# Macaron block: VectorE's routing passes spread over more units, low parts of two groups of units on other engines, three weight pieces ahead

## What is computed

```python
x = x + 0.5 * ffn(layernorm(x))      # x: 2048 tokens x 128
x = x + attention(layernorm(x))
x = x + 0.5 * ffn(layernorm(x))

def ffn(x):                           # 64 experts, D = 128, F = 64
    shared = silu(x @ Ws_up) @ Ws_down
    aff = x @ centroids.T
    _, idx = top_k(aff + expert_biases, 8)
    w = sigmoid(take(aff, idx)); w = w / (sum(w) + 1e-8)
    cw = zeros(T, 64) with w at idx
    h = silu(einsum('td,edf->etf', x, W_up))
    y = einsum('etf,efd->etd', h, W_down)
    return shared + einsum('etd,te->td', y, cw)

def attention(x):                     # one head of 128, 2048 x 2048 logits
    q, k, v = x @ Wq, x @ Wk, x @ Wv
    return (softmax(q @ k.T) / sqrt(128)) @ v
```

## Time and profile before

| what | us |
|---|---|
| median of 3 runs | 564.39 (564.20 to 564.67) |
| the profiled execution, its own time | 564.02 |
| its span, first to last instruction | 562.2 |
| PE busy | 536.9 (95%) |
| VectorE busy | 409.1 (73%) |
| ScalarE busy | 411.1 (73%) |
| GpSimd busy | 274.5 (49%) |
| granted TensorE clock, mean | 0.993 |

### The profile page before, as it was taken

How to read it: one execution, slowest core, us unless ns; L and a number is a source line. 1 busy time by engine, 2 the same in 40 slices (tenths; PEclk the granted TensorE clock), 3 DMA queues, 4 the chain that set the end, 5 groups by cost and what they waited for, 6 DMA issues and landing times.

```text
span 562.2 us, 8626 instructions
## 1 busy us (share of the span) xinstructions
PE 536.9 (95%) x2683; PEld 436.3 (78%) x2683; DVE 409.1 (73%) x920; ACT 411.1 (73%) x814; POOL 274.5 (49%) x242
## 2 busy tenths in 40 slices
PE   7699999899989999999999999899999999999997
PEld 5476887688778887679999999777787788778885
DVE  5478678867876775676778979687777967875664
ACT  7688877777787786666666656677877787787774
POOL 3897675676676675100000000064775666567563
PEclk9799999999999999999999999999999999999999
DMA  8544664455446562000000000054565466466652
GB/s 267 178 152 149 196 206 154 149 181 169 147 149 196 183 192 60 0 1 2 1 2 0 2 1 1 2 158 151 178 198 178 150 193 189 145 183 196 196 189 97
DMA packets 44270, 72.25 MB, mean 129 GB/s; under 512 B 8864, under 2 KB 9632, under 8 KB 44224
## 3 DMA queue, kind: packets, MB, share of 16 engines
q1 hardware_dynamic: 43568, 71.17, 39.7%
q10 hardware_dynamic: 592, 0.39, 0.2%
q0 software_dynamic: 64, 0.13, 0.1%
HBM read 69.57 MB, written 2.10 MB: 127 GB/s over the span
## 4 chain that ended last, share of the span: by engine, by line
PE 76%; DVE 9%; ACT 6%; issue 4%; POOL 3%; DMA 1%; POOLq 0%; SPq 0%; DVEq 0%; ACTq 0%
PE lrow L1044 11%; PE lrow L1045 11%; PE lrow L1046 11%; PE bank L1082 9%; PE bank L1084 8%; PE bank L1083 8%; PE bank L1116 6%; PE bank L1316 3%; PE bank L1318 3%; PE bank L1317 3%; ACT gpart_hi L437 2%; DVE rec L754 2%; ACT lrow L426 1%; POOL gpart_lo L273 1%; DVE gpart_lo L273 1%
## 5 line engine op out<-in xcount | busy, mean ns | idle before, releaser
L273 POOL TENSOR_TENSOR gpart_lo<-gated,gpart_hi 128x512 fp32r<-128x512 f32 x174 | 224.9, 1295 | 183.3 <-ACT gpart_hi L437 179.3
L426 ACT ACTIVATE lrow<-lrow 128x512 f32<-128x512 f32 (+1 forms) x246 | 143.6, 584 | 60.3 <-PE lrow L1046 60.1
L670 DVE TENSOR_TENSOR gated<-lrow,wide 128x512 f32<-128x512 f32 x166 | 114.2, 688 | 47.9 <-ACT lrow L426 44.8
L437 ACT CAST gpart_hi<-gated 128x512 fp32r<-128x512 f32 x174 | 106.7, 614 | 13.1 <-DVE gated L670 12.6
L1082 PE MATMUL bank<-gpart_lo,wdn_hi 128*128 128x512 f32 x256 | 102.3, 399 | 5.7 <-POOL gpart_lo L273 5.7
L1084 PE MATMUL bank<-gpart_hi,wdn_hi 128*128 128x512 f32 x256 | 101.8, 398 | 0.0
L1083 PE MATMUL bank<-gpart_hi,wdn_lo 128*128 128x512 f32 x256 | 101.3, 396 | 0.0
L670 DVE TENSOR_TENSOR lrow<-lrow,wide 128x512 f32<-128x512 f32 x78 | 54.3, 696 | 41.6 <-ACT lrow L426 41.3
L1082 PEld LDWEIGHTS bank<-gpart_lo,wdn_hi 128*128 128x128 f32 x256 | 48.3, 189 | 19.4 <-issue 5.6
L979 DVE TENSOR_TENSOR pT_lo<-bank,pT_hi 128x512 fp32r<-128x512 f32 x64 | 43.7, 684 | 25.7 <-ACT pT_hi L614 25.7
L273 DVE TENSOR_TENSOR gpart_lo<-lrow,gpart_hi 128x512 fp32r<-128x512 f32 (+1 forms) x84 | 57.4, 683 | 2.5 <-ACT gpart_hi L437 1.8
(11 more groups left out here) (239 smaller groups left out, 943.6 us busy)
## 6 DMA issues: line engine op xcount, KB each, us to landing
wide<-gates_dram SPq DMA_DIRECT2D x488, 128.0 KB, 3.0
raw<-in_w_up SPq DMA_DIRECT2D x8, 256.0 KB, 5.5
raw<-in_w_down SPq DMA_DIRECT2D x8, 256.0 KB, 5.7
gates_dram<-gates SPq DMA_DIRECT2D x8, 128.0 KB, 2.3
x<-in_x SPq DMA_DIRECT2D x3, 256.0 KB, 3.6
out_dram<-x SPq DMA_DIRECT2D x3, 256.0 KB, 2.9
x<-in_x SPq DMA_DIRECT2D x1, 128.0 KB, 2.7
x<-in_x ACTq DMA_DIRECT2D x1, 128.0 KB, 2.9
```

The source lines that it names most:

```text
L273: return eng.tensor_tensor(gpart[1][0:m, U % NGP, :], gated_at(U)[0:m, :], gpart[0][0:m, U % NGP, :].bitcast(F32), ALU.subtract)
L426: nc.scalar.activation(dst[0:m, :], hid[U % NH][0:m, :], ACT.Silu).then_inc(s_silu, 1)
L437: nc.scalar.copy(gpart[0][0:m, U % NGP, :], gated_at(U)[0:m, :]).then_inc(s_ghi, 1)
L670: nc.vector.tensor_tensor(gated_at(U), a, b, ALU.mult).then_inc(s_gated, 1)
```

## The change

- **First chunk.** `PRE` is 3, so three weight pieces are made ahead and the others at units 0, 2, ... 24. ScalarE makes a unit's conversion before the piece in the same step, and piece 2 before the gates' copy. In chunk 0 up to unit 24, `on_pool` gives GpSimd only units 7, 9, ... 23; VectorE makes the low parts of units 0 to 6 and of the even ones. The small products for attention's weights come three units later.
- **Routing passes.** The reciprocal is two halves of two token tiles each, behind `pro_aff` at unit 14 and behind unit 15's gate; GpSimd's `weights` waits for both through a new semaphore. `joint_lo` moves from unit 15 to 24. Attention's normalisation moves from units 17 and 18 to 20 and 21, with its scratch in the free down bank. kT's steps move from 22 and 23 to 26 and 27, qT's from 26 and 27 to 30, 31 and 32, the values from 24 to 27, and attention's `rstd` on GpSimd from 14 to 12.
- **Unit 15** of every chunk has its low part on GpSimd.

```diff
-PRE = 6
+PRE = 3
@@ on_pool
-            return u % 3 != 0 and (u < UNITS - 1 or n % NCH < NCH - 1)
+            if n == 0 and u < 25:
+                return u > EARLY and u % 2 == 1
+            return u == 15 or u % 3 != 0 and (u < UNITS - 1 or n % NCH < NCH - 1)
@@ GpSimd
+                pool.wait_ge(p_rec, 2 * joint(n))
                 pool.wait_ge(p_top, n + 1)
...
-                        if f == 0 and c and u == 14:
+                        if f == 0 and c and u == 12:
                             rstd(1, c - 1, e_st, e_rs)
-                        if f == 0 and c and u == 24:
+                        if f == 0 and c and u == 27:
                             value_parts(c - 1)
@@ ScalarE
+                            piece_hi(2)
                             pro_cwT(n)
-                            piece_hi(2)
                             silu_unit(3, n)
-                            for k in range(3, PRE):
-                                piece_hi(k)
...
+                        if c or u > 1 - f:
+                            hi_unit(*before(u, n))
                         if n == 0 and u % 2 == 0 and PRE + u // 2 < 2 * WP:
                             piece_hi(PRE + u // 2)
-                        if c or u > 1 - f:
-                            hi_unit(*before(u, n))
@@ VectorE
+                free = yacc[n % 2] if k else mp
+                ve, t, r = (free[:, TPC * E + i * TPC:TPC * E + (i + 1) * TPC] for i in range(3))
...
+            def reciprocal(n, half):
+
+                dve.wait_ge(p_affs, n)
+                some = slice(half * GT, (half + 1) * GT)
+                nc.vector.reciprocal(rec[:, some, :], aff[n // NCH][:, some, :]).then_inc(p_rec, 1)
...
                                 pro_aff(n + 1, 1)
+                                reciprocal(n + 1, 0)
                             if u == 15:
-                                pro_top(n + 1, 0)
+                                reciprocal(n + 1, 1)
+                            if u == 24:
                                 joint_lo(n + 1)
...
-                                if u == 17:
+                                if u == 20:
...
-                                if u == 18:
+                                if u == 21:
                                     normed(1, c - 1, c - 1, xn2, e_rs, e_xn, (2, 3))
-                                if u == 23:
+                                if u == 27:
                                     epi_lo(c - 1)
-                                if u == 27:
+                                if u == 32:
                                     epi_proj_lo(c - 1)
@@ TensorE
-                                if u == 22:
+                                if u == 26:
                                     epi_xT(c - 1)
-                                if u == 26:
+                                if u == 30:
                                     epi_proj(c - 1)
```

More of the change, by code:

```diff
@@ L157, in macaron_kernel @@
         j_out, j_aff, j_silu, j_hi, j_lo = (sem("shared_" + n) for n in ("and_aff", "aff_copied", "silu", "hi", "lo"))
+        p_rec = sem("p_reciprocal")
         s_pad = sem("wsdn_pad_zeroed")
@@ L577, in _ @@
                                 epi_y(n - 1)
-                            if f == 0 and u == 23:
+                            if f == 0 and u == 27:
                                 epi_hi(c - 1)
-                            if f == 0 and u == 27:
+                            if f == 0 and u == 31:
                                 epi_proj_hi(c - 1)
@@ L583, in _ @@
                             turned_hi()
-                        if n == 0 and u == 16:
+                        if n == 0 and u == 19:
                             qk_hi()
@@ L695, in normed @@
             def normed(k, n, c, dst, ready, done, tiles):
-                ve, t, r = (mp[:, TPC * E + (3 * k + i) * TPC:TPC * E + (3 * k + i + 1) * TPC] for i in range(3))
+                free = yacc[n % 2] if k else mp
+                ve, t, r = (free[:, TPC * E + i * TPC:TPC * E + (i + 1) * TPC] for i in range(3))
                 if 0 in tiles:
                     dve.wait_ge(ready, n + 1)
-                    dve.wait_ge(s_gates, n if k == 0 else n + 2)
+                    dve.wait_ge(e_y if k else s_gates, n + k)
                     link(nc.vector.tensor_scalar(ve, mv[:, k, :, 1], EPS, None, ALU.add))
@@ L951, in _ @@
                             turned_lo()
-                        if n == 0 and u == 17:
+                        if n == 0 and u == 20:
                             qk_lo()
@@ L1265, in _ @@
                             turn_weights()
-                        if n == 0 and u == 15:
+                        if n == 0 and u == 18:
                             qk_weights()
```

## The result

| | us |
|---|---|
| before, median of 5 runs beside it | 564.24 (563.89 to 564.67) |
| after, median of 5 runs | 549.87 (549.50 to 551.69) |
| ratio, 95% interval | 0.9753 (0.9742 to 0.9763) |
| profiled executions, own time | 564.02 and 549.50 |
| their spans | 562.2 and 547.7 |

The change takes 14.4 us off the median, 2.5%; 14.3 were forecast. The prediction of 550.1 us is 0.2 us off, and its sizes stretch by stretch came out nearly as put.

A forecast was written before the change was run, and what follows sets the result against it. PE, busy 95% of the span, was taken as the bound, so only its waits and lower clock pay: 5.5 + 1.0 + 5.5 + 2.4 - 0.1 = 14.3 us off 564.02, 549.7, or 550.1 as median; range 547.6 to 555.

The forecast's parts named there:

- The start: First chunk up to unit 9's up product: PE's 4.50 us wait for GpSimd's low part of unit 1 shrinks, gain 5.5 us.
- The walk: Hand trace of the engine queues in chunk 0 from 16.30 us, putting unit 9's up product at 26.3, before 31.79.
- The clock: Start of chunk 0: ten matmuls slowed by PE's lower granted clock, 0.19 us each, 1.9 us to win.
- Rival (a): Start of chunk 0: the lower clock stays, so the 1.9 us are not won, 552.0 us; chance 0.13.
- The rest of chunk 0: Units 9 to 25 of chunk 0: gain taken as 1.0 us, between 2.3 and a loss of 2.
- Chunks 1 and 2: PE's waits at units 19 and 22 for VectorE's low parts both go: 2.75 us a chunk, 5.5 us for two.
- rival (c): Chunks 1 and 2: the waits move to unit 25, half of 1.78 returns twice, 551.9 us; chance 0.12.
- Chunks 4 to 6: One PE wait in each, at unit 19, goes: 0.81 us three times, 2.4 us.
- Chunk 3's last Silu: Chunk 3: qT's high part (0.5 us) stands in front of the last Silu, 0.1 to 0.2 us lost.
- Rival (b): Chunk 0: ScalarE or VectorE becomes the bound; 1.0 becomes a loss of 2, start loses a microsecond, 554 us; chance 0.17.
- Rival (d): Chunk 0: GpSimd's pair of low part and piece takes 4.4 us, not 2.8; about 564.5 us or more; chance 0.03.
- Rival (e): Start gains held back as something else paces chunk 0, such as gates from memory; only 7.9 us remain, 556.5; chance 0.06.

## Why the prediction was right, point by point

**The start: 5.5 forecast, 5.2 measured, and 0.2 of luck.** The walk put unit 9 at 26.3, and it came at 26.41. But 0.22 us of the difference to before lies ahead of the changed code, in when VectorE finishes `cw2` (13.60 to 14.30 us in the kernels run here). Measured from there, 5.16 us are the change's. The walk missed the subtraction held up by GpSimd, 0.65 us; the earlier start, and 0.16 us that VectorE had waited there before, hid most of it, so that the first gate starts at 16.50 where the walk had 16.30. From there every step of the walk comes about 0.2 us late and no more: low part 4 ends at 22.89 (22.7 in the walk), low part 5 at 25.41 (25.2), the last normalised tile at 25.93 (25.75). Which part of the change does it was put too broadly: with GpSimd making the low parts as before, unit 9 comes at the same time. The three pieces ahead, with ScalarE's order, are enough.

**The clock.** Its 1.9 us were won in full: 1.00 in place of 0.67 and 0.65 in the windows of 20 to 30 us. Rival (a) is out. PE had waits of 0.33, 0.21 and 0.42 us between 17 and 27 us, and none of them was followed by matmuls at the slow spacing; the one of 4.50 us before was.

**The rest of chunk 0: 1.0 forecast, 1.1 measured, the reason only half right.** The walk named two waits, unit 22 for low part 18 and the gates' transposes for GpSimd. Both are there, with 0.29 us and 0.65 us lost from start to start where I had 0.45 + 0.27 each. Two loads were miscounted: in this stretch GpSimd gives up three low parts, not two, and is busy 20.86 us where I had about 22, and ScalarE gets two more pieces, not three (24.23 us and not 24.6). And I booked the 1.0 us to the denser first chunk as if the routing part were a separate thing there. It isn't: without the routing part the stretch would have lost 0.6 us and not won 1.1. What the split reciprocal (0.8) and the later shared low part (0.9) are worth lies mostly in chunk 0; the low parts by odd and even units (2.05) are worth something only behind the start. The hand walk was made with the queues as they stand after, so its number came out right; the sentences that shared it out did not. The two waits were put at 1.4 us together and cost 0.94; without them the stretch takes 24.96 us, 0.25 more than the floor of 24.7 that I had taken.

**Chunks 1 and 2: 2.75 forecast, 2.73 measured.** Both waits are gone. The attribution was too generous to unit 15's low part (nothing by itself, 0.5 if the reciprocal is whole) and to the shared low part (0.25 and 0.29), and nearer with the normalisation (0.70 a chunk; the larger wait was 1.78). Taken back one at a time the edits give 1 us of the 2.73 a chunk; the rest shows only when several go together. The thin cover of 0.7 us at unit 25 held, so rival (c) is out.

**Chunks 4 to 6: 2.4 forecast, 2.69 measured,** 0.09 us a chunk more. The wait of unit 19 gave 0.80 of the 0.81 that were put. What I had missed is a second, small wait in the same chunks: in the profile before, the weight load of unit 22 in chunk 4 waits for the low part of unit 18, and the matmuls of that up product start 0.33 us apart once in place of 0.23. It has gone after.

```profile
395.81 0.19 PEld L1044 LDWEIGHTS lrow<-xnT_lo_b,wup_hi 128*128 128x128 f32 x1 [0.27 <-DVE gpart_lo L273]
```

The later shared low part alone removes the wait of unit 19, and so do the two other edits together.

**Chunk 3's last Silu:** 0.1 to 0.2 us of loss forecast, 0.06 measured. **GpSimd's price for unit 15:** nothing, as put; nothing gained either.

**Rival (b)** was near. ScalarE has 24.23 of 25.91 us in the stretch and still doesn't hold PE up. **Rival (d)** would have needed 4.4 us a pair on GpSimd; it was busy 20.86 of 25.91 us. With the old low parts in chunk 0 GpSimd does become the bound, and the price is 2 us, not 14. **Rival (e)** is out with the start.

**What stays open.** Why the `cw2` subtraction comes anywhere between 13.60 and 14.30 us wasn't tried. Nor was PRE = 3 without ScalarE's new order, so how much of the start each of them wins isn't shown.

## What to carry to other kernels

Price a regrouped queue by walking it in its final order, and don't share the sum out among the edits before each has been taken back alone: here one edit earned nothing, two earned their keep in another chunk than the one they were made for, and 2.2 us belonged to the two parts together. Look for work that a slow helper engine does ahead of time (six pieces of 1.24 us) in front of the first thing that the bound engine needs; moving three of the pieces behind won 5 us at the start, a third of it through the clock by the estimate of 1.9 us. It wasn't free: until VectorE took low parts over, the rest of chunk 0 was 1 us longer than before (39.27 us and 38.29). When the big waits are gone, list what PE still waits for in order of time; three such waits of 0.3 to 0.65 us gave the last 1.4 us of chunk 0.

## What the runs showed of the hardware

A VectorE subtraction of 64x128 elements with both inputs in SBUF takes 0.29 us alone, 0.94 us when it starts 0.48 us into a low part on GpSimd, and 1.28 us when it starts 0.16 us into one; both times it ends 0.15 us after GpSimd's instruction. The two rows of the kernel after:

```profile
15.12 0.94 DVE L894 TENSOR_TENSOR wsdn_pad<-rawd,wsdn_hi 64x128 fp32r<-64x128 f32 x1
```

```profile
14.64 1.27 POOL L363 TENSOR_TENSOR wup_lo<-raw,wup_hi 128x512 fp32r<-128x512 f32 x1 [1.20 <-ACT wup_hi L510]
```

VectorE's low parts and gates, which have one input in PSUM, keep their 0.68 us beside the same GpSimd work. The profile before had this already, and I overlooked it. A step in making chunk 0's gates, a multiplication of 128x48 elements with both inputs in SBUF, takes 0.80 us at 12.94, beside GpSimd's low part of a weight piece (12.40 to 13.67), and ends 0.06 us after it. The same instruction takes 0.21 us for chunk 4's gates, with GpSimd idle:

```profile
12.94 0.80 DVE L822 TENSOR_TENSOR rest<-rec,wsum 128x48 fp32r<-128x48 f32 x1
...
359.19 0.21 DVE L822 TENSOR_TENSOR rest<-rec,wsum 128x48 fp32r<-128x48 f32 x1
```

```profile
12.40 1.27 POOL L360 TENSOR_TENSOR wdn_lo<-raw,wdn_hi 128x512 fp32r<-128x512 f32 x1 [2.83 <-ACT wdn_hi L506]
```

It is 0.79 to 1.15 us long in every kernel run here, and the `cw2` subtraction, for which PE waits, stands two instructions behind it. Some 0.6 us at the start may lie there, an estimate from 0.80 less 0.21; no kernel here tried it.
The Trainium skill (SBUF — State Buffer, section SBUF: two separate sides) states it: a VectorE instruction with two SBUF inputs and a GpSimd instruction that reads SBUF take an exclusive lock in turn, and the one that comes later waits. The trace agrees. A list of waits doesn't show this kind, since the time stands in the instruction's own duration. Moving either of the two away gives the 0.65 us back to VectorE; 0.4 us of it reached PE when the subtraction was moved, none when GpSimd's piece was.
